# State space loop: the second state's output products move from VectorE and TensorE to GpSimd, and three orders around the cross attention change

## The reference, cut to what matters

```python
# _L0_attn_ref, state space block: d_inner 512, d_state 16
delta = softplus(einsum('blr,er->ble', dt, W_dt) + b_dt)
dA = exp(delta[..., None] * A)
dBx = delta[..., None] * Bm[:, :, None, :] * xc[..., None]
h = dA_t * h + dBx_t                       # along time, for each of 16 states
y = einsum('bles,bls->ble', hs, Cm) + xc * Dp
# _L1_xattn_ref: 16 heads, 2 x 128 queries, 4096 keys
q, k = _fq_sym(q, -1), _fq_sym(k, -1); v = _fq_sym(v, 2)
attn = _fq_unsigned(softmax(einsum('bhqd,bhkd->bhqk', q, k)), -1)
out = einsum('bhqk,bhkd->bqhd', attn, v)
```

## Time and profile before

| | us |
|---|---|
| three runs | 444.31, 444.06, 440.26 |
| median | 444.06 |
| the profiled execution, whole | 442.38 |
| its span in the profile | 440.6 |

### The profile page before, as it was taken

The page is one execution under the profiler, slowest core; times in us unless marked ns, Lnnn a source line. Parts: engine busy times, 40 slices in busy tenths (PEclk is TensorE's granted clock), DMA queues, the critical chain, the costliest instruction groups (busy, mean ns, idle before and its releaser), DMA issues.

```text
span 440.6 us, 9345 instructions
## 1 busy us (share of the span) xinstructions
PE 408.4 (93%) x3822; PEld 297.9 (68%) x3822; DVE 357.3 (81%) x582; ACT 303.0 (69%) x382; POOL 105.3 (24%) x177
## 2 busy tenths in 40 slices
PE   8989899999999999999789999999999999888897
PEld 4878778855555554576347777777777777755686
DVE  2846662879999999987899999999999999654343
ACT  3245834788888776553789999999999999811110
POOL 3100402044444444001245333321111111100000
PEclk9999999999999999999989999999999999889899
DMA  7898912411001100369488789999999894300000
GB/s 281 295 425 301 196 70 73 192 32 31 25 27 27 31 3 0 140 227 438 210 243 249 251 274 263 243 255 251 250 220 311 203 273 101 51 1 0 1 1 24
DMA packets 48245, 71.46 MB, mean 162 GB/s; under 512 B 38954, under 2 KB 41674, under 8 KB 42698
## 3 DMA queue, kind: packets, MB, share of 16 engines
q1 hardware_dynamic: 47626, 67.32, 51.4%
q0 software_dynamic: 576, 3.54, 2.1%
HBM read 61.58 MB, written 1.15 MB: 142 GB/s over the span
## 4 chain that ended last, share of the span: by engine, by line
PE 43%; DVE 41%; issue 7%; ACT 4%; DMA 3%; SPq 1%; DVEq 0%; ACTq 0%
DVE arena L1387 20%; DVE w L1387 9%; PE ps L1671 6%; PE ps L1781 5%; PE ps L1680 5%; PE ps L2058 4%; DVE arena L1398 3%; PE ps L1564 2%; PE ps L1628 2%; DMA arena<-in_segg 2%; PE ps L1720 2%; PE ps L2069 2%; PE ps L1588 1%; PE ps L1493 1%; PE ps L1837 1%
## 5 line engine op out<-in xcount | busy, mean ns | idle before, releaser
L1387 DVE CUSTOM_DVE_ANT_0 arena<-ps,arena 128x1024 f32<-128x1024 f32 x88 | 107.5, 1277 | 0.1
L1897 PE MATMUL ps<-arena 128*128 128x512 bf16 x256 | 77.6, 384 | 11.0 <-DVE arena L1387 7.4
L1002 ACT ACTIVATE arena<-arena 128x4096 uint8<-128x4096 f32 x21 | 78.0, 3716 | 7.8 <-POOL arena L697 7.8
L1921 PEld LDWEIGHTS ps<-cst,arena 128*128 128x128 f32 x384 | 48.2, 144 | 23.2 <-ACT arena L1002 7.2
L1921 PE MATMUL ps<-cst,arena 128*128 128x128 f32 x384 | 59.8, 280 | 2.7 <-ACT arena L1017 2.1
L1941 PE MATMUL ps<-vrow,arena 128*128 128x16 f16 x806 | 52.6, 170 | 0.5 <-ACT w L1017 0.5
L1941 PEld LDWEIGHTS ps<-vrow,arena 128*128 128x128 f16 x806 | 49.2, 96 | 3.9 <-ACT w L1017 0.6
L1387 DVE CUSTOM_DVE_ANT_0 w<-ps,arena 128x1024 f32<-128x1024 f32 x40 | 49.6, 1276 | 0.0
L1944 PE MATMUL ps<-vrow,arena 128*128 128x16 f16 x768 | 45.8, 170 | 0.0
L672 POOL TENSOR_TENSOR arena<-arena 128x1024 f32<-128x1024 f32 x14 | 33.0, 2358 | 39.2 <-DVE arena L1276 39.2
L1944 PEld LDWEIGHTS ps<-vrow,arena 128*128 128x128 f16 x768 | 40.9, 98 | 1.4 <-DVE arena L1398 0.3
(11 more groups left out here) (278 smaller groups left out, 743.8 us busy)
## 6 DMA issues: line engine op xcount, KB each, us to landing
arena<-ks_scr SPq DMA_DIRECT2D x32, 1024.0 KB, 5.6
arena<-in_w SPq DMA_DIRECT2D x1, 4488.0 KB, 22.1
arena<-in_columns SPq DMA_DIRECT2D x4, 1024.0 KB, 7.8
arena<-in_w0b SPq DMA_DIRECT2D x1, 2560.0 KB, 16.7
w<-in_w SPq DMA_DIRECT2D x1, 2286.0 KB, 10.8
arena<-in_w SPq DMA_DIRECT2D x1, 2048.0 KB, 7.7
arena<-in_fill SPq DMA_DIRECT2D x1, 2048.0 KB, 9.1
arena<-bc_scr SPq DMA_DIRECT2D x14, 128.0 KB, 3.0
```

Of the source, the lines that this page charges most:

```text
L1002: act.activation(out8[:, :, 0], s_sb[u % 3], ACT.Exp, bias=nb[:, u % 3:u % 3 + 1], accum_out=zall[:, u:u + 1]).then_inc(p_ready, 1)
L1387: dve.tensor_tensor_reduce(s_sb[slot][:, keys], ps[:, 2 * (c % 2):2 * (c % 2) + 2, :].rearrange("p a n -> p (a n)"), ksb[h % 2][:, keys], ...
L1897: mm = pe.matmul(bank(2 * (c % 2) + m, 0, 512), qz[h // 8][:, h % 8, b * L:(b + 1) * L], kT[:, h // 8, k:k + 512], start=True, stop=True)
L1921: mm = pe.transpose(bank(4 + n % 3, k * P, P), words[:, w:w + P], ident)
```

## The change

- In the loop, VectorE's `read_out(i, 1)` is left only for the last pair. For pairs 0 to 6 GpSimd makes the product of `hst[:, 1]` and the C row (`second_product`), and adds it to a running sum in SBUF (`running_sum`, from pair 1 on). Seven products and six sums of 128x1024.
- The C row for it comes by a DMA on SP's queue into `bcc` (two slots), behind the B row of odd `n`: seven more DMAs.
- `input_of(i + 1, 0)` now waits for `h_ready` 2i+1, the first scan of the pair, in place of 2i+2. `input_of(i + 1, 1)` waits as before.
- `scan(i, 1)` waits for GpSimd's product of the pair before (`hp_made`) in place of VectorE's.
- VectorE's order becomes scan 0, scan 1, read_out 0, key_maxima, largest, scaled_keys.
- TensorE sums up only state 0 of each pair, broadcasts one C row in place of two, and adds GpSimd's running sum once, between the sum of the last pair's two products.
- `on_vector`: VectorE takes chunk 0 of units with `u % 2 == 0` in place of `u % 3 < 2`.
- ScalarE's Exp table load moves ahead of `columns(3, 0)`; TensorE's order becomes `columns(3, 1)`, `queries(1)`, `query_columns(0)`, `value_rows(2)`.

```diff
 def on_vector(u, c):
-    return (u % 3 < 2 or u >= LAST - 1) if c == 0 else (...)
+    return (u % 2 == 0 or u >= LAST - 1) if c == 0 else (...)
+def products(i):
+    return max(1, 2 * i)
...
+        hp = early[:, 0:3 * ET * T].rearrange("k (s t n) -> k s t n", s=3, t=ET)
+        bcc = early[:, 3 * ET * T:3 * ET * T + 2 * T].rearrange("k (s n) -> k s n", s=2)
...
+                if n % 2:
+                    i = (n - 3) // 2
+                    if i >= 2:
+                        sp.wait_ge(hp_made, products(i - 2))
+                    sp.dma_start(bcc[:, i % 2, :], bc_scr[2 * i + 1:2 * i + 2, 1, :]....).then_inc(ld_b[n % 4], 16)
...
             def input_of(i, s):
-                pool.wait_ge(h_ready, 2 * i)
+                pool.wait_ge(h_ready, max(2, 2 * i - 1 + s))
+            def second_product(i):
+                n = 2 * i + 3
+                pool.wait_ge(ld_b[n % 4], 32 * ((n + 2) // 4))
+                pool.wait_ge(h_ready, 2 * i + 2)
+                if i >= 2:
+                    pool.wait_ge(hp_made, 2 * i - 1)
+                pool.tensor_tensor(hp[:, i % 2 if i else 2], hst[:, 1, :]...., bcc[:, i % 2, :]...., ALU.mult).then_inc(hp_made, 1)
+            def running_sum(i):
+                pool.wait_ge(hp_made, 2 * i)
+                pool.tensor_tensor(hp[:, 2], hp[:, 2], hp[:, i % 2], ALU.add).then_inc(hp_made, 1)
             for i in range(NC - 1):
                 input_of(i + 1, 0)
+                second_product(i)
                 if i + 2 < NC:
                     scales_of(i + 2)
                 input_of(i + 1, 1)
+                if i:
+                    running_sum(i)
...
+            act.activation(spare[:, :], spare[:, :], ACT.Exp)
             columns(3, 0)
-            act.activation(spare[:, :], spare[:, :], ACT.Exp)
...
             def scan(i, s):
                 if i:
-                    dve.wait_ge(hc_made, 2 * i - 1 + s)
+                    if s == 0:
+                        dve.wait_ge(hc_made, i)
+                    else:
+                        dve.wait_ge(hp_made, products(i - 1))
...
                 read_out(i, 0)
+                if i == NC - 1:
+                    read_out(i, 1)
                 if i + 2 < NC:
                     key_maxima(i + 2)
-                read_out(i, 1)
+                largest(i)
                 if i + 2 < NC:
                     scaled_keys(i + 2)
-                largest(i)
...
+            def sum_of_products():
+                pe.wait_ge(hp_made, products(6) + 1)
+                summed(hp[:, 2])
...
-                sum_of(i, 0).then_inc(hc_used[0], 1)
-                sum_of(i, 1).then_inc(hc_used[1], 1)
+                sum_of(i)
...
-            sum_of(NC - 1, 0)
-            pe.wait_ge(hc_made, 2 * NC)
+            sum_of(NC - 1)
+            sum_of_products()
+            pe.wait_ge(hc_made, NC + 1)
...
             columns(3, 1)
+            queries(1)
+            query_columns(0)
             value_rows(2)
-            query_columns(0)
-            queries(1)
```

## The result

| | before | after |
|---|---|---|
| runs of the first comparison, median (us) | 444.19 (440.26 to 445.43) | 460.74 (459.87 to 462.78) |
| ratio, 95% interval | | 1.0395 (1.0322 to 1.0468) |
| profiled execution, whole | 442.38 | 462.78 |
| its span | 440.6 | 461.0 |

The change makes the kernel slower, by 16.6 us in the medians and 20.4 in the two profiled executions. A second comparison gave a ratio of 1.0471 (1.0374 to 1.0567), with 464.77 against 441.95.

What follows compares the result with a forecast made beforehand. It took TensorE to bound the old loop and scans plus GpSimd the new: +23.5 + 1.7 + 1.7 - 3.0 - 1.3 = +22.6 on 442.38 gives 465.0; the median, 1.7 above, was named 466, range 453 to 474.

Steps and rivals of the forecast that it cites:

- One track for scans and GpSimd: In the loop, scans and GpSimd's work exclude each other, so their times add to 14.14 us per iteration against 11.04.
- rival 1: In the loop, a running scan doesn't hold GpSimd up; a period of 9.75 and 434 us in all; chance 9%.
- Rival 2: In the loop, only half of the scans' time counts for GpSimd; period 11.95, 449 us in all; chance 5%.
- +23.5 for the loop: The loop's last scan would end at 200.8 in place of 177.3 us.
- Nothing for what TensorE and ScalarE save: In the loop, their savings hide under the shared track of scans and GpSimd and are worth nothing.
- So the loop is TensorE's by 0.4 us: In the kernel before, TensorE's period of 11.04 us bounds the loop, with VectorE's 10.61 right behind.
- +3.4 behind the loop: After the last scan: +1.7 us for one more sum on TensorE and +1.7 for its lower clock.
- -3.0 for `on_vector`: In the cross attention, VectorE takes 15 first chunks instead of 20, five times 0.60 us less; bounds -3.0 and +2.
- -1.3 for the orders: Ahead of the cross attention, the 1.30 us wait before batch 1's queries are rounded goes; bound 0.
- Rival 3: As forecast, but the attention gives nothing and the clock stays low through the last sums; 472 us; chance 12%.

Runs made afterwards that it cites:

- awake_44: The changed kernel with 44 filler matmuls in place of 18 ahead of the last sums: 458.44 us, 1.0419 of the kernel before.
- after_again: The changed kernel measured once more without further change, as the yardstick: 464.77 us, 1.0471 of the kernel before.
- loop_edits: The changed kernel without its three edits around the cross attention: 465.05 us, 1.0568 of the kernel before.
- wait_both_scans: The changed kernel with `input_of` waiting for both scans of the pair before, as it did: 464.57 us.
- orders_only: The kernel before with only the two reorderings ahead of the cross attention: 439.16 us, 0.9977 of the kernel before.
- the edits alone: The kernel before with only the three edits around the cross attention: 435.49 us, 0.9898 of the kernel before.

## Why the prediction was right

The forecast was 466 (453 to 474), the time 460.74. In the profiled executions it was 465.0 and 462.78. Its steps:

- **One track for scans and GpSimd: right.** Its open half, that a running scan also holds a GpSimd product, is shown by the products of 4.33 us under scans, and rival 1 (434) falls with it. Rival 2, that half of the scans' time counts, needed a period of 11.95; of 13.62 less GpSimd's 9.75, 3.87 of the scans' 4.39 us counted. The run with the operand from PSUM shows that it hangs on the scan's second SBUF operand.
- **+23.5 for the loop: 3.2 too much.** The term that was off is the price of a held instruction. I set 0.13 less for each, 2 in all, and let handovers eat it up. A scan and the product held by it take 4.30 together from start to start (136.75 to 141.05), not 4.54, and there are two such in a period: 13.62 instead of 14.14. Handovers cost nothing that shows. The running sum, the one unseen price, takes 2.34 when not held, as assumed; that both its operands are whole arrays made no difference.
- **Nothing for what TensorE and ScalarE save: right.** TensorE waits in every period for the key bias, 0.5 to 4.2 us (14.3 in five on the page); from 122.61 to 177.09 it was busy 43.90 of 54.48 us, so it idled 2.6 per period and not near 5. Its granted clock over these four periods was 0.87, which I had reckoned with only behind the loop: three of five groups of sixteen key matmuls took 5.25, 6.33 and 6.36 us, the other two 3.72. The periods of 13.62 don't show it, since GpSimd's track is the longer.
- **"So the loop is TensorE's by 0.4 us": wrong, at no cost to the sum.** In the kernel before, VectorE's pairs start 10.60 us apart (10.72 the last time), its list of waits is empty between 98 and 178 us, and it is its last scan that ends the loop at 177.3. TensorE, at 11.04, falls behind it without ever stopping it. The bar for a new period was therefore 10.6 and not 11.04, for rival 1 too. The term of the loop is a difference of two scan ends and doesn't use the bar.
- **+3.4 behind the loop: 1.15 too little.** The further sum was 1.7 (5.76 with the clock at 1.00 in awake_44, against 4.05 before). The clock cost 2.85 by the two traces and 2.5 by the run with 44 fillers, where I had put 1.7 with bounds of 0 and 5.2; TensorE had waited 6.7 us, not 10. The size differs between executions: last scan to first gate took 8.60, 8.23, 7.46 and 7.30 us in four traces with this code (after, after_again, loop_edits, wait_both_scans), 1.5 to 2.85 above awake_44.
- **-3.0 for `on_vector`: right.** 5.12 us a unit as worked out, -3.1 from the first maxima to the last. It holds over all traces: 165.07 to 166.60 us with the old choice of units (before, loop_edits, orders_only), 161.97 to 163.35 with the new. **-1.3 for the orders:** -1.1, since a wait of 0.24 stays.
- **The base.** By traces the change costs 20.4, the forecast said 22.6; part of that nearness is luck, since the loop's -3.2 and the +1.15 behind it offset each other. The medians differ by 16.6 in the first comparison and by 22.8 in the second, and the kernel before itself has medians of 444.19, 441.95, 440.10 and 439.22. I put that down to the variation behind the attention; I had taken no account of it.

Rival 3, an attention that gives nothing, is out by the trace and by the edits alone. Its sum had a slip: 442.38 + 1.7 + 29.1 is 473, not 472, still within the range.

## What to carry to other kernels

Before work is moved to an idle GpSimd, look in the trace for VectorE instructions with two SBUF operands in the same stretch, and add their time to that of GpSimd's instructions that read SBUF: here the two lists were one queue. A single outlier in a line's min/median/max (3.68 among scans of 2.28) was enough to see one direction, a scan held by a GpSimd product. The other, which decides between 434 and 466, stood in no row of this pair and was taken over. A balance by engine, 9.2, 9.4 and 9.75 us here, each under the old 10.6, was worth nothing without that sum, which gave 14.1; 13.6 were measured.

Before two profiles are compared, cut them at marks in the code. A stretch that the change doesn't touch can differ by more than the effect looked for, as the last 60 us do here.

## What the runs showed that I had not expected

- A held instruction is cheaper than a free one, by 0.2 to 0.3 us: 4.33 for a scan of 2.28 and a product of 2.34 behind it. Letting GpSimd start early and be held beat waiting by semaphore by 0.33 us a pair (13.62 against 13.95), in one trace of each.
- TensorE's granted clock behind the cross attention differs from execution to execution of the same kernel (0.92 and 0.86 over the last 63 and 65 us), and over twelve traces it goes with a length of that stretch from 59.4 to 64.9 us, more than the edits around the attention give.
